# A second edge pass with two sum tables, the last matrix product moved behind the sums, and half of the one-hots on GpSimd

## The chip, the cores and the metric

One core of one Trainium2 chip runs the whole program. The metric is the device time of one execution in microseconds (us). The kernel before has a median of 10212.68 us over 3 runs (10212.11 to 10216.0).

## What is computed

Four graph layers follow one another on 6250 nodes and 106250 edges (100000 drawn ones and a loop per node), each followed by a layer norm of `x + layer(x)`. Only the third layer is touched here:

```python
ef = jnp.concatenate([x[row], x[col], edge_attr], axis=-1)
h = ef @ W1 + b1                              # one row of 128 per edge
mu = jnp.mean(h, axis=0)
var = jnp.mean((h - mu) ** 2, axis=0)
h = (h - mu) * jax.lax.rsqrt(var + BN_EPS) * gamma + beta
h = jax.nn.relu(h)
msgs = h @ W2 + b2
sums = jax.ops.segment_sum(msgs, row, num_segments=n_nodes)
counts = jax.ops.segment_sum(jnp.ones((msgs.shape[0],), dtype=msgs.dtype), row, num_segments=n_nodes)
out = sums / (counts + 1.0)[:, None]
return out + x
```

## The kernel before

The third layer works on edges sorted by source node. Every tile of 128 edges lies inside one block of 128 source nodes; there are 880 tiles, 16 in an iteration (55 iterations, `ITERS2`), and four tiles make a quad. A first pass, `edge_hidden`, computes `h` for every edge, stores it channel by edge in the DRAM table `t_hidden`, and collects the moments. `batch_norm_rows` turns the moments into one scale and one shift per channel. The second pass, `scatter_by_source`, is the one that is changed; then `after_block2` finishes the layer and prepares the fourth one.

In the second pass every quad `q` goes through five steps, each on its own engine, tied by semaphores:

- SP loads 8 tiles (two quads) of `t_hidden` into `rows`, one buffer for each half of the iteration (L2004).
- ACT applies scale, shift and ReLU to the four tiles of a quad (`activate`, L2011), and later copies the quad's messages from PSUM to SBUF (`keep`, L2017).
- PE multiplies each tile by W2, which turns it to edge by channel (`layer`, L2077), and then multiplies it by the tile's one-hot, edge by node of the block, which sums the messages of each node (`add_up`, L2086).
- DVE makes the four one-hots of a quad in one comparison of 128x512 (`match`, L2040), and adds the four 128x128 results to the table `summed` at the column where the tile's node block begins (`add`, L2052). Neighbouring tiles often belong to the same block, so every add waits for the one before it.
- The columns come from `bases`, which loads eight of them at once into DVE's registers (L484), twice in an iteration, ahead of the comparison of that quad.

The order on each engine is written out by hand. DVE: [bases], match(q+1), add(q). ACT: activate(q+1), keep(q). PE: layer(q+1), add_up(q). PSUM holds two quads of each kind, so add_up(q) waits for the adds of quad q-2. GpSimd is idle in this pass.

`after_block2` goes over 7 groups of 7 blocks. DVE joins the sums, the bias times the count, the division and `x` (L2136 to L2143) and runs the layer norm (L820 to L834, its square root on ACT, L841); PE turns the rows (L2195), makes the root product (L2201) and 14 banks of messages (L2208); ACT copies the rows (L2165, L2168), the root product (L2170) and the banks (L2157) and issues the store of the group to DRAM (L2174), for whose end the next group's bank copies wait.

Of the kernel before, what the change touches and what calls it, by code (L numbers as in the profile page):

```python
# [1978 lines left out]
def scatter_by_source(nc, m, a):  # L1979

    with ExitStack() as ctx:
        sb, pb, sem = place(nc, ctx, "sc")
        w2 = sb("w2", [P, C])
# [7 lines left out]
        relued, made, kept, hot_ready, added, window_used = (  # L1991
            [sem(f"{n}{q}") for q in range(QUADS)] for n in ("relued", "made", "kept", "hot_ready", "added", "window_used"))
        w_in, cleared = sem("w_in", "cleared")
        block = ctx.enter_context(nc.Block())
        places = m.iota[:].rearrange("p (a n) -> p a n", a=1).to_broadcast([P, QU, P])

        @block.sync
        def _(sp):
            sp.dma_start(w2[:], a["L2_gnn_W2"]).then_inc(w_in, 16)
# [7 lines left out]
        def _(act):  # L2007
# [10 lines left out]

            activate(0, 0)
# [11 lines left out]

        @block.vector
        def _(dve):
            nc.vector.memset(m.summed[:], 0.0).then_inc(cleared, 1)
            dve.wait_ge(cleared, 1)

            def match(it, q):
                dve.wait_ge(added[q], it)
                low = m.low[:, bass.ds(it * U + q * QU, QU)].rearrange("p (t a) -> p t a", a=1).to_broadcast([P, QU, P])
                nc.vector.tensor_tensor(hot[:, q], places, low, ALU.is_equal).then_inc(hot_ready[q], 1)  # L2040

            def add(it, q, base):
# [21 lines left out]
            for q in range(QUADS):  # L2064
                if q % 2 == 0:
                    base = bases(nc, m.block_base, (ITERS2 - 1) * U + q * QU, DVE, (NT - 1) * P)
                if q < QUADS - 1:
                    match(ITERS2 - 1, q + 1)
# [341 lines left out]
```

## Time and profile before

| | us |
|---|---|
| median of 3 runs | 10212.68 |
| the profiled execution, its own time | 10201.99 |
| its span | 10199.8 |
| second edge pass, loop and ends (8373.0 to 8924.3 of the span) | 551 |
| `after_block2` (8924.3 to about 9095) | 171 |

Engine shares over the whole span: PE 66%, DVE 50%, ACT 13%, GpSimd 66%. They are averages over stages with different limits, so the stage of the change is read by itself. Times in rows are from the span's start; a row's mean duration covers an instruction from start to end, while the next one on the same engine may start before that end, so a pace is read from the distance of starts.

### The profile page before, as it was taken

Reading aid. Unit: us, or ns where it says so; the run is one execution under the profiler, and the core shown is the slowest. Engines: PE = TensorE matmul, PEld = TensorE weight load, DVE = VectorE, ACT = ScalarE, POOL = GpSimd, SP = SyncE. Lnnn points to the kernel's source line nnn. Section 1 sums busy time; section 2 is a strip of 40 time slices with the busy share of each in tenths; the row PEclk is TensorE's granted clock in tenths of the full one; section 3 lists DMA queues with packets and bytes.
Section 4 is the critical chain, followed back from the end, with each engine's and each line's share of the span. In section 5 each row is a group of like instructions: output and inputs, shape, how many; then the busy total and the mean of one; then the engine's idle time right before and its main releaser. Section 6 shows DMA issues by size and latency. Waiting matters only on the chain. (4 is left out here: it accounts for less than half of the span.)

```text
span 10199.8 us, 143982 instructions
## 1 busy us (share of the span) xinstructions
PE 6706.4 (66%) x31287; PEld 5127.7 (50%) x31287; DVE 5144.5 (50%) x16272; ACT 1308.2 (13%) x3084; POOL 6692.3 (66%) x7546
## 2 busy tenths in 40 slices
PE   2787755556677896705888746665566668866665
PEld 1666533334566654404777524444455557733343
DVE  6555655554455534665777434444222226644445
ACT  0000000000000015700000100001122225530000
POOL 1777647777777777767777777773577750027775
PEclk8666655556666685557999955556677779975555
DMA  1222112222333330004777512222566663332222
GB/s 53 52 52 52 45 49 50 51 51 62 98 104 104 104 106 17 2 10 138 220 219 220 169 35 52 52 52 55 146 187 184 185 148 106 100 121 52 52 52 53
DMA packets 556744, 932.76 MB, mean 91 GB/s; under 512 B 161514, under 2 KB 336326, under 8 KB 556302
## 3 DMA queue, kind: packets, MB, share of 16 engines
q0 software_dynamic: 271264, 606.93, 22.5%
q1 hardware_dynamic: 279038, 299.48, 9.4%
q10 hardware_dynamic: 6384, 25.69, 0.6%
q8 instruction: 22, 0.36, 0.0%
q14 instruction: 36, 0.29, 0.0%
HBM read 788.54 MB, written 143.03 MB: 91 GB/s over the span
## 5 line engine op out<-in xcount | busy, mean ns | idle before, releaser
L728 PE MATMUL sage_window<-sage_hot,sage_message 128*128 128x128 f32 x4992 | 1450.2, 433 | 751.7 <-DMA sage_message<-t_x,sage_index_stage 307.2
L728 PEld LDWEIGHTS sage_window<-sage_hot,sage_message 128*128 128x128 f32 x4992 | 1087.5, 297 | 1114.5 <-issue 615.6
L728 PE MATMUL block_window<-block_hot,block_message 128*128 128x128 f32 x3328 | 1186.8, 457 | 672.6 <-DMA block_message<-t_rel,block_index_stage 345.3
L728 PEld LDWEIGHTS block_window<-block_hot,block_message 128*128 128x128 f32 x3328 | 787.3, 294 | 1047.3 <-issue 657.5
L668 DVE TENSOR_TENSOR first_acc<-first_acc,sage_window 128x128 f32 (+1 forms) x1664 | 590.9, 355 | 874.2 <-PE sage_window L728 867.7
L1871 POOL DMA_INDIRECT eh_message<-t_q,eh_stage x880 | 832.2, 946 | 251.9 <-issue 233.9
L578 POOL DMA_INDIRECT sage_message<-t_x,sage_index_stage x832 | 817.4, 982 | 237.6 <-issue 222.1
L728 PE MATMUL gat_window<-gat_hot,gat_message 128*128 128x128 f32 x6656 | 848.0, 281 | 187.7 <-DVE gat_hot L586 96.8
L578 POOL DMA_INDIRECT gat_message<-t_h,gat_index_stage x832 | 793.6, 954 | 237.5 <-issue 222.1
L578 POOL DMA_INDIRECT sage_message<-t_s,sage_index_stage x832 | 788.9, 948 | 237.5 <-issue 222.1
L578 POOL DMA_INDIRECT rgcn_message<-t_rel,rgcn_index_stage x832 | 788.8, 948 | 237.5 <-issue 222.1
L578 POOL DMA_INDIRECT block_message<-in_x,block_index_stage x832 | 787.3, 946 | 237.5 <-issue 222.0
L578 POOL DMA_INDIRECT block_message<-t_rel,block_index_stage x832 | 786.9, 946 | 237.6 <-issue 222.1
L728 PE MATMUL rgcn_window<-rgcn_hot,rgcn_message 128*128 128x128 f32 x1664 | 614.3, 480 | 463.3 <-DMA rgcn_message<-t_rel,rgcn_index_stage 295.3
L728 PEld LDWEIGHTS gat_window<-gat_hot,gat_message 128*128 128x128 f32 x6656 | 782.5, 192 | 249.3 <-issue 106.2
L577 POOL TENSOR_TENSOR all_carrier<-all_ones_i 1x1 int32<-1x1 int32 x624 | 124.4, 199 | 1138.2 <-ACT block_index_stage L565 947.2
L728 PEld LDWEIGHTS rgcn_window<-rgcn_hot,rgcn_message 128*128 128x128 f32 x1664 | 415.1, 313 | 657.9 <-issue 492.2
L1924 PE MATMUL eh_ps<-eh_hot,eh_window 128*128 128x128 f32 x1760 | 481.2, 367 | 389.5 <-DMA eh_message<-t_q,eh_stage 377.7
L1908 DVE TENSOR_SCALAR_CACHE_REDUCE eh_hot<-eh_low_rows,all_column 128x128 f32<-128x128 bf16 x880 | 243.4, 342 | 883.2 <-DMA eh_low_rows<-t_low 883.2
L1924 PEld LDWEIGHTS eh_ps<-eh_hot,eh_window 128*128 128x128 f32 x1760 | 377.3, 265 | 463.8 <-issue 457.5
L784 POOL DMA_INDIRECT t_rec<-attention_records,all_position x420 | 455.0, 1083 | 192.4 <-issue 128.9
L586 DVE TENSOR_SCALAR gat_hot<-all_iota,all_rel,all_alpha 128x128 f32<-128x128 f32 x1680 | 518.5, 362 | 69.6 <-issue 69.5
(474 smaller groups left out, 11121.3 us busy)
## 6 DMA issues: line engine op xcount, KB each, us to landing
eh_window<-t_p SPq DMA_DIRECT2D x880, 64.0 KB
t_hidden<-eh_hidden SPq DMA_DIRECT2D x110, 512.0 KB
sc_rows<-t_hidden SPq DMA_DIRECT2D x110, 512.0 KB, 3.6
eh_low_rows<-t_low SPq DMA_DIRECT2D x110, 256.0 KB, 3.5
t_rel<-n_h ACTq DMA_DIRECT2D x7, 3584.0 KB
eh_message<-t_q,eh_stage POOLq DMA_INDIRECT x880
block_message<-in_x,block_index_stage POOLq DMA_INDIRECT x832, 2.5
sage_message<-t_x,sage_index_stage POOLq DMA_INDIRECT x832, 2.5
```

Source lines behind the costliest of these rows:

```text
L577: nc.gpsimd.tensor_tensor(m.carrier[:], m.ones_i[:], m.ones_i[:], ALU.add).then_inc(e.carried, 1)
L578: pool.indirect_dma_start(message[u][:], None, table, bass.IndirectOffsetOnAxis(ap=stage[h][:, k:k + 1], axis=0)).then_inc(e.gathered[u], 16)
L586: ins = nc.vector.tensor_scalar(hot[:, u, k * P:(k + 1) * P], m.iota[:], m.rel[:, t], weights[k][:, t], ALU.is_equal, ALU.mult)
L668: nc.vector.tensor_tensor(window, window, ps[k][:], ALU.add).then_inc(e.window_used, 1)
L728: last = nc.tensor.matmul(ps[k][:, b, :], message[u][:, f:f + P], hot[:, u, j * P:(j + 1) * P], start=(j == 0), stop=(j == heads - 1))
L784: pool.indirect_dma_start(m.t_rec, bass.IndirectOffsetOnAxis(ap=m.position[:, t0 + n:t0 + n + 1], axis=0), records[:, n, :], None).then_in ...
L1871: pool.indirect_dma_start(message[:, u, :], None, m.t_q, bass.IndirectOffsetOnAxis(ap=stage[h][:, k:k + 1], axis=0)).then_inc(gathered[u / ...
L1908: nc.vector.tensor_scalar(hot[:, q, e], rows, m.column[:], 0.0, ALU.is_equal, ALU.add, accum_out=m.of_source[:, bass.ds(it * U + q * QU + ...
L1924: nc.tensor.matmul(ps[q][:, e], window[:, u, :], hot[:, q, e], start=False, stop=False, skip_group_check=True)
```

## The change

Four edits to the second pass, and what they need in `after_block2`:

- Tiles 0 and 2 of a quad add to `summed`, tiles 1 and 3 to a second table `of_odd`; an add waits for the one two places before it. A second memset clears `of_odd`, and one addition over 128x6272 joins the tables at the end.
- W2 is applied to the summed rows: in the pass PE only turns each tile (`turn`), and `add_up` has its operands exchanged, so that the tables hold channel by node. In `after_block2` ACT copies a group of sums (`first`), PE multiplies its seven blocks by W2 (`project`), and DVE reads the products from PSUM. W2 is loaded there.
- `bases` is issued behind `match` of the same quad instead of ahead of it.
- DVE compares two tiles of a quad (128x256); GpSimd makes the other two, one instruction of 128x128 each, from a copy of eight keys that ACT makes for each half (`stage`), behind a 1x1 addition on `m.carrier`.

```diff
+            def stage(it, h):
+                for q in (2 * h, 2 * h + 1):
+                    act.wait_ge(hot_pool[q], 2 * it)
+                nc.scalar.copy(low[:, h], m.low[:, bass.ds(it * U + h * HU, HU)]).then_inc(staged[h], 1)
...
                     keep(it, q)
+                    if q % 2 == 1:
+                        stage(it + 1, q // 2)
...
+        @block.gpsimd
+        def _(pool):
+            with pool.Fori(0, ITERS2, 1) as it:
+                for q in range(QUADS):
+                    pool.wait_ge(carried, it * QUADS + q)
+                    pool.wait_ge(staged[q // 2], it + 1)
+                    pool.wait_ge(added[q], it)
+                    nc.gpsimd.tensor_tensor(m.carrier[:], m.ones_i[:], m.ones_i[:], ALU.add).then_inc(carried, 1)
+                    for k in range(2, QU):
+                        u = q % 2 * QU + k
+                        nc.gpsimd.tensor_scalar(hot[:, q, k], m.iota[:], low[:, q // 2, u:u + 1], None, ALU.is_equal).then_inc(hot_pool[q], 1)
+
         @block.vector
         def _(dve):
             nc.vector.memset(m.summed[:], 0.0).then_inc(cleared, 1)
-            dve.wait_ge(cleared, 1)
+            nc.vector.memset(of_odd[:], 0.0).then_inc(cleared, 1)
+            dve.wait_ge(cleared, 2)
 
             def match(it, q):
                 dve.wait_ge(added[q], it)
-                low = m.low[:, bass.ds(it * U + q * QU, QU)].rearrange("p (t a) -> p t a", a=1).to_broadcast([P, QU, P])
-                nc.vector.tensor_tensor(hot[:, q], places, low, ALU.is_equal).then_inc(hot_ready[q], 1)
+                key = m.low[:, bass.ds(it * U + q * QU, 2)].rearrange("p (t a) -> p t a", a=1).to_broadcast([P, 2, P])
+                nc.vector.tensor_tensor(hot[:, q, 0:2], places, key, ALU.is_equal).then_inc(hot_dve[q], 1)
 
             def add(it, q, base):
                 dve.wait_ge(added[q], it + 1)
                 for k in range(QU):
-                    if k == 0 and q == 0:
+                    if k < 2 and q == 0:
                         dve.wait_ge(window_used[QUADS - 1], QU * it)
-                    elif k == 0:
-                        dve.wait_ge(window_used[q - 1], QU * (it + 1))
+                    elif k < 2:
+                        dve.wait_ge(window_used[q - 1], QU * it + 3 + k)
                     else:
-                        dve.wait_ge(window_used[q], QU * it + k)
-                    window = m.summed[:, bass.ds(base[(q % 2) * QU + k], C)]
-                    nc.vector.tensor_tensor(window, window, ps_a[q % 2][:, k, :], ALU.add).then_inc(window_used[q], 1)
+                        dve.wait_ge(window_used[q], QU * it + k - 1)
+                    table = (m.summed, of_odd)[k % 2]
+                    nodes = table[:, bass.ds(base[(q % 2) * QU + k], C)]
+                    nc.vector.tensor_tensor(nodes, nodes, ps_a[q % 2][:, k, :], ALU.add).then_inc(window_used[q], 1)
...
                 for q in range(QUADS):
-                    if q % 2 == 0:
-                        base = bases(nc, m.block_base, it * U + q * QU, DVE, (NT - 1) * P)
                     if q < QUADS - 1:
                         match(it, q + 1)
                     else:
                         match(it + 1, 0)
+                    if q % 2 == 0:
+                        base = bases(nc, m.block_base, it * U + q * QU, DVE, (NT - 1) * P)
                     add(it, q, base)
...
+            dve.wait_ge(window_used[QUADS - 1], QU * ITERS2)
+            chain(dve, m)(nc.vector.tensor_tensor(m.summed[:], m.summed[:], of_odd[:], ALU.add))
 
         @block.tensor
         def _(pe):
-            def layer(it, q):
+            def turn(it, q):
                 pe.wait_ge(relued[q], it + 1)
                 pe.wait_ge(*bank_before(kept, it, q))
                 for k in range(QU):
-                    last = nc.tensor.matmul(ps_m[q % 2][:, k, :], relu[:, q, k * P:(k + 1) * P], w2[:], start=True, stop=True)
+                    last = nc.tensor.transpose(ps_m[q % 2][:, k, :], relu[:, q, k * P:(k + 1) * P], m.ident[:])
                 last.then_inc(made[q], 1)
...
-                    last = nc.tensor.matmul(ps_a[q % 2][:, k, :], hot[:, q, k, :], message[:, q, k, :], start=True, stop=True)
+                    last = nc.tensor.matmul(ps_a[q % 2][:, k, :], message[:, q, k, :], hot[:, q, k, :], start=True, stop=True)
                 last.then_inc(added[q], 1)
...
-                    nc.vector.scalar_tensor_tensor(y[:, j, :], b2[:], m.out_degree[:, 0, node], m.summed[:, bass.ds((g * GN + j) * C, C)],
+                    nc.vector.scalar_tensor_tensor(y[:, j, :], b2[:], m.out_degree[:, 0, node], ps[:, j, :],
                                                    ALU.mult, ALU.add).then_inc(joined, 1)
...
+            def first(g):
+                act.wait_ge(made, g)
+                nc.scalar.copy(sums[:].rearrange("p j n -> p (j n)"), m.summed[:, group_cols(g)]).then_inc(staged, 1)
...
             with act.Fori(0, NG - 1, 1) as g:
+                first(g + 1)
                 take(g, range(EARLY))
...
+            def project(g):
+                pe.wait_ge(staged, g + 1)
+                pe.wait_ge(root_taken, g)
+                for j in range(GN):
+                    last = nc.tensor.matmul(ps[:, j, :], sums[:, j, :], w2[:], start=True, stop=True)
+                last.then_inc(made, 1)
...
+            project(0)
             root_term(0)
             with pe.Fori(0, NG - 1, 1) as g:
+                project(g + 1)
                 messages(g)
                 root_term(g + 1)
```

## Rows read from the trace of the kernel before

**Rows 1.** Stretches, loop of the pass and `after_block2`: PE, PEld, DVE, ACT, POOL busy; clock

```profile
8383.50:8921.40 537.90, 444.24 (x3496) 406.35 (x3494) 373.66 (x1095) 281.46 (x435) 0.00 (x0) 1.00 0.36 104
8929.30:9095.00 165.70, 116.26 (x273) 52.88 (x273) 64.51 (x271) 75.59 (x128) 0.18 (x2) 0.86 0.38 155
```

**Rows 2.** Groups by line, 8377 to 8925: count, busy us, mean ns, idle before

```profile
L2052 DVE TENSOR_TENSOR by_source_summed<-by_source_summed,sc_ps_a 128x128 f32 x880 | 251.8, 286 | 89.0 <-PE sc_ps_a L2086 2.2 <-DVE by_source_summed L2052 0.2
L2086 PE MATMUL sc_ps_a<-sc_message,sc_hot 128*128 128x128 f32 x1760 | 251.2, 286 | 93.2 <-issue 74.2 <-DVE sc_hot L2040 18.9
L2077 PE MATMUL sc_ps_m<-sc_w,sc_relu 128*128 128x128 f32 x1760 | 234.1, 276 | 6.9 <-ACT sc_relu L2011 6.9
...
L2011 ACT ACTIVATE sc_relu<-sc_rows,all_norm 128x512 f32<-128x512 f32 x220 | 179.4, 816 | 11.0 <-DMA sc_rows<-t_hidden 11.0
L2040 DVE TENSOR_TENSOR sc_hot<-all_iota,edges_low 128x512 f32<-128x512 f32 x220 | 151.4, 688 | 78.0 <-issue 78.0
L2017 ACT COPY sc_message<-sc_ps_m 128x512 f32<-128x512 f32 x220 | 128.7, 585 | 254.8 <-PE sc_ps_m L2077 254.8
```

**Rows 3.** Instructions in order of time, DVE, one iteration: start, duration

```profile
8601.75 0.69 DVE L2040 TENSOR_TENSOR sc_hot<-all_iota,edges_low 128x512 f32<-128x512 f32 x1
8602.35 1.54 DVE L2052 TENSOR_TENSOR by_source_summed<-by_source_summed,sc_ps_a 128x128 f32 x4
8604.46 0.69 DVE L2040 TENSOR_TENSOR sc_hot<-all_iota,edges_low 128x512 f32<-128x512 f32 x1 [0.57 <-issue]
...
8609.53 0.69 DVE L2040 TENSOR_TENSOR sc_hot<-all_iota,edges_low 128x512 f32<-128x512 f32 x1 [0.86 <-issue]
```

**Rows 4.** One line's instructions (L484) in that iteration, min/median/max ns

```profile
L484 DVEq TENSOR_LOAD <-edges_block_base x2: 595/596/596, 8603.7 to 8608.8; - x2
```

**Rows 5.** In order of time, PE, the loop's first quads

```profile
8384.13 1.06 PE L2086 MATMUL sc_ps_a<-sc_message,sc_hot 128*128 128x128 f32 x8
8385.02 1.06 PE L2077 MATMUL sc_ps_m<-sc_w,sc_relu 128*128 128x128 f32 x8
```

**Rows 6.** In order of time, PE: seven transposes at granted clock 1.00, seven at about 0.5

```profile
8957.72 0.93 PE L2195 MATMUL n_ps_t<-all_ident,n_x 128*128 128x128 f32 x7
...
8364.94 1.73 PE L1972 MATMUL bn_ps_t<-all_ident,edges_of_source 128*128 128x128 f32 x7 [6.80 <-PEq L799]
```

**Rows 7.** In order of time, DVE: an unchained addition from PSUM and its follower

```profile
3706.45 0.28 DVE L1232 TENSOR_TENSOR n_f_out<-n_ps_fa,first_sage_bias_f 128x128 f32<-128x128 f32 x1
3706.64 0.15 DVE L1233 COPY all_al<-n_ps_fa 128x4 f32<-128x4 f32 x1
```

**Rows 8.** One line's instructions: DVE comparison of two SBUF inputs, min/median/max ns

```profile
L1376 DVE TENSOR_TENSOR al_high_hot<-all_iota,all_src_high x208: 350/352/415, 3900.9 to 4314.8; 128x196 f32<-128x196 f32 x104
```

**Rows 9.** One line's instructions, GpSimd: the 1x1 addition and an indirect DMA

```profile
L1870 POOL TENSOR_TENSOR all_carrier<-all_ones_i x110: 181/181/183, 7225.2 to 8326.8; 1x1 int32<-1x1 int32 x110
L1871 POOL DMA_INDIRECT eh_message<-t_q,eh_stage x880: 940/944/967, 7225.8 to 8336.2; - x176
```

**Rows 10.** One line's instructions: landing of the row loads (L2004); ACT copy 128x8

```profile
DMA to landing us min/median/max: 3.4/3.6/4.4
L1877 ACT COPY eh_stage<-edges_dst x110: 192/195/197, 7224.9 to 8326.5; 128x8 int32 x108, 128x8 int32<-128x8 int32 x2
```

**Rows 11.** One line's instructions: whole-table operations on DVE

```profile
L2034 DVE MEMSET by_source_summed<- x1: 5285/5285/5285, 8374.5 to 8374.5; 128x6272 f32 x1
L882 DVE TENSOR_TENSOR degrees_ends<-degrees_ends,all_ident x1: 6692/6692/6692, 1279.3 to 1279.3; 128x6272 f32<-128x6272 f32 x1
```

**Rows 12.** In order of time, ACT and PE in `after_block2`, one group

```profile
8986.69 0.91 ACT L2170 COPY third_acc<-n_ps 128x896 f32 x1 [3.43 <-PE n_ps L2201]
8991.25 3.24 ACT L2157 COPY n_h<-n_ps_h 128x512 f32<-128x512 f32 x6 [3.66 <-DMA t_rel<-n_h]
8991.89 8.85 PE L2208 MATMUL n_ps_h<-n_w,n_x_t 128*128 128x512 f32 x20 [1.68 <-ACT n_h L2157]
```

**Rows 13.** Stretch of the first edge pass, columns as in rows 1

```profile
7400.00:7500.00 100.00, 64.94 (x344) 55.48 (x343) 22.20 (x160) 26.16 (x90) 76.99 (x91) 0.78 0.63 188
```

More of the change, by code:

```diff
@@ L1982, in scatter_by_source @@
         sb, pb, sem = place(nc, ctx, "sc")
-        w2 = sb("w2", [P, C])
         rows = sb("rows", [P, 2, HU * P])
@@ L1990, in scatter_by_source @@
         rows_in = [sem(f"rows_in{h}") for h in range(2)]
-        relued, made, kept, hot_ready, added, window_used = (
-            [sem(f"{n}{q}") for q in range(QUADS)] for n in ("relued", "made", "kept", "hot_ready", "added", "window_used"))
-        w_in, cleared = sem("w_in", "cleared")
+        low, of_odd = sb("low", [P, 2, HU]), sb("of_odd", [P, ROWS])
+        relued, made, kept, hot_dve, hot_pool, added, window_used = (
+            [sem(f"{n}{q}") for q in range(QUADS)] for n in ("relued", "made", "kept", "hot_dve", "hot_pool", "added", "window_used"))
+        staged = [sem(f"staged{h}") for h in range(2)]
+        cleared, carried = sem("cleared", "carried")
         block = ctx.enter_context(nc.Block())
-        places = m.iota[:].rearrange("p (a n) -> p a n", a=1).to_broadcast([P, QU, P])
+        places = m.iota[:].rearrange("p (a n) -> p a n", a=1).to_broadcast([P, 2, P])
         @block.sync
         def _(sp):
-            sp.dma_start(w2[:], a["L2_gnn_W2"]).then_inc(w_in, 16)
             with sp.Fori(0, ITERS2, 1) as it:
@@ L2017, in keep @@
                 nc.scalar.copy(message[:, q], ps_m[q % 2][:]).then_inc(kept[q], 1)
+            def stage(it, h):
+                for q in (2 * h, 2 * h + 1):
+                    act.wait_ge(hot_pool[q], 2 * it)
+                nc.scalar.copy(low[:, h], m.low[:, bass.ds(it * U + h * HU, HU)]).then_inc(staged[h], 1)
+            for h in range(2):
+                stage(0, h)
             activate(0, 0)
@@ L2062, in _ @@
                         match(it + 1, 0)
+                    if q % 2 == 0:
+                        base = bases(nc, m.block_base, it * U + q * QU, DVE, (NT - 1) * P)
                     add(it, q, base)
             for q in range(QUADS):
+                if q < QUADS - 1:
+                    match(ITERS2 - 1, q + 1)
                 if q % 2 == 0:
                     base = bases(nc, m.block_base, (ITERS2 - 1) * U + q * QU, DVE, (NT - 1) * P)
-                if q < QUADS - 1:
-                    match(ITERS2 - 1, q + 1)
                 add(ITERS2 - 1, q, base)
+            dve.wait_ge(window_used[QUADS - 1], QU * ITERS2)
+            chain(dve, m)(nc.vector.tensor_tensor(m.summed[:], m.summed[:], of_odd[:], ALU.add))
         @block.tensor
         def _(pe):
-            def layer(it, q):
+            def turn(it, q):
                 pe.wait_ge(relued[q], it + 1)
@@ L2081, in add_up @@
                 pe.wait_ge(kept[q], it + 1)
-                pe.wait_ge(hot_ready[q], it + 1)
+                pe.wait_ge(hot_dve[q], it + 1)
+                pe.wait_ge(hot_pool[q], 2 * (it + 1))
                 used, times = bank_before(window_used, it, q)
@@ L2085, in add_up @@
                 for k in range(QU):
-                    last = nc.tensor.matmul(ps_a[q % 2][:, k, :], hot[:, q, k, :], message[:, q, k, :], start=True, stop=True)
+                    last = nc.tensor.matmul(ps_a[q % 2][:, k, :], message[:, q, k, :], hot[:, q, k, :], start=True, stop=True)
                 last.then_inc(added[q], 1)
-            pe.wait_ge(w_in, 16)
-            layer(0, 0)
+            turn(0, 0)
             with pe.Fori(0, ITERS2 - 1, 1) as it:
@@ L2093, in _ @@
                     if q < QUADS - 1:
-                        layer(it, q + 1)
+                        turn(it, q + 1)
                     else:
-                        layer(it + 1, 0)
+                        turn(it + 1, 0)
                     add_up(it, q)
@@ L2099, in _ @@
                 if q < QUADS - 1:
-                    layer(ITERS2 - 1, q + 1)
+                    turn(ITERS2 - 1, q + 1)
                 add_up(ITERS2 - 1, q)
@@ L2174, in store @@
                 act.dma_start(node_rows(m.t_rel8, g, R8 * C), h[:].rearrange("p j r n -> p j (r n)")).then_inc(stored, 16)
+            first(0)
             second(0)
```

8 lines of the change are left out of this document (5 added, 3 removed).

## The prediction

> **What bounds the kernel now.** The page's shares (PE 66%, DVE 50%) say nothing about this stage, so I read the stretches first. In the loop of the second edge pass PE is busy 444 of 538 us at a granted clock of 1.00, DVE 374, ACT 281, GpSimd none [rows 1]. PE looks like the bound. The groups by line correct that: the adds on DVE waited for PE 2.2 us in all, and the 78 us before comparisons and most of the 89 us between adds have no other engine behind them, while PE idled 93 us before `add_up` [rows 2]. DVE in order of time settles it [rows 3]: a comparison starts at 8601.75, its quad of adds at 8602.35, and the next comparison at 8604.46, where it sat idle 0.57 us; at the loop's end it is 0.86. From 8601.75 to the same place an iteration later are 9.84 us. So DVE is the bound, through latency as much as work: four adds take 1.54 us, 4 x 0.286 of work and three gaps of 0.13 [rows 2, 3] where an add waits for the one before. The two longer idles hold a register load of 0.596 us [rows 4] that starts at 8603.7, with the last add, and at 8608.8.
>
> The profiled execution took 10201.99 us, the median is 10212.68: I make the sum against the first and add the 10.7 at the end.
>
> **The change part by part.** I work out an iteration of 16 tiles for every engine; the longest counts, and all else is paid once or in `after_block2`.
>
> *DVE, adds.* An add that waits for the one two places back may start when that has ended, 0.286 + 0.13 = 0.42 us after its start, so two adds share 0.42. Unchained, such an addition from PSUM is followed after 0.19 us [rows 7]. Both give 0.21 an add, 0.84 a quad against a start-to-start 1.45 now (8602.35 plus 1.54, less the overlap of 0.09 with the next comparison). Bounds: 0.19, and 0.42 if they still ran one by one.
>
> *DVE, comparisons.* 128x512 takes 0.69, the next instruction follows after 0.60 [rows 3]; 128x196 takes 0.35 [rows 8], so an element costs 0.00107 us, and 128x256 takes 0.42, followed after 0.34. A quad is 0.34 + 0.84 = 1.18 us, four are 4.7.
>
> *DVE, bases behind the comparison.* The load needs 0.6 us of the sequencer and started about 0.1 after the last add. Behind `match` it starts a little later but runs while that add and the comparison (0.21 + 0.34) execute; the adds need it. What stays uncovered is about 0.4 us in mid-iteration and 0.65 at the loop's branch, where the load starts 0.3 later. The two now cost 0.65 and 0.95 (9.84 less four times 2.06 of a plain quad). DVE: 4.7 + 1.05 = 5.8 us an iteration.
>
> *PE.* Unhindered, four matmuls (eight records) start 0.89 us after the previous four [rows 5]. Seven transposes take 0.93 us at full clock, one record each, so 0.11 us a transpose [rows 6]: `turn` is 0.45. A quad is 1.34, an iteration 5.4 (now 7.1). The exchange of operands in `add_up` changes no size; I cost it at nothing.
>
> *ACT.* ReLU 0.816 and copy 0.585 [rows 2] overlap their followers by 0.1 each, 1.2 us a quad; two stagings of 0.195 [rows 10] come on top: 5.2 us. `stage` waits for GpSimd's previous use of the keys; queued behind that wait are the next ReLU, the copy PE waits for, and so all of it, if GpSimd lags. An iteration's distance should cover it.
>
> *GpSimd.* No compute instruction of size runs on it in this trace. Below lies the 1x1 addition of 0.181, above the indirect DMA of 0.944 [rows 9]. DVE does a 128x128 addition in 0.286. I take 0.5, between the small one and twice DVE's: a quad is 0.181 + 2 x 0.5 + 0.15 for waits, about 1.3, an iteration 5.3. By the ends it is 2.8 or 8.9. The Trainium skill (GPSIMD Engine Reference, side-by-side cycle accounting) has about 2.6 cycles an element at 1.2 GHz, by which the work of 128 columns would be an estimated 0.28 us and the instruction near 0.46; no run here shows it.
>
> *DVE against GpSimd.* Comparisons on DVE while GpSimd is busy with DMA issues ran 350/352/415 ns [rows 8], so hardly a delay, but GpSimd read nothing from SBUF there. I leave 0 to 0.3 us a comparison and take 0.1. The Trainium skill (SBUF: two separate sides) says that a DVE instruction with two SBUF inputs and a GpSimd instruction that reads SBUF exclude one another for their whole length. The comparison has two such inputs; by that rule an average wait could be 0.12 us and the worst 0.5; the row cannot decide it.
>
> *The row loads.* A half's buffer is reloaded when ReLU has consumed it, and a load lands 3.6 us after issue (3.4 to 4.4) [rows 10]. Now three quads (7.4 us) hide that. After the change a cycle of the buffer is 0.2 + 3.6 + 0.1 for load and hand-over, then 0.7 + 0.5 + 0.2 + 0.8 of ReLU, copy, staging, ReLU: 6.1 us. This is late next together with DVE.
>
> So DVE has 5.8 + 0.4 = 6.2, the loads 6.1, PE 5.4, GpSimd 5.3, ACT 5.2. With that many near one another I add 0.3 for them missing each other: 6.5 us, in a plausible band of 5.8 to 7.2. Saved: 55 x (9.84 - 6.5) = 184 us (145 to 222).
>
> *Paid once.* The second memset stands before the first comparison: 5.3; the joining addition has the size of L882: 6.7, and 0.2 for its wait [rows 11]. Together 12.2.
>
> *after_block2.* Group 0 now begins with an ACT copy of 128x896 (0.91 [rows 12]), 7 matmuls at half clock (7 x 0.44) and hand-overs: 4.3. In the first loop pass PE can start its messages only behind copy and product (0.9 + 7 x 0.22 + hand-overs, perhaps part at half clock): 3.5. In the other five ACT waits 3.66 us for the store anyway, which hides copy and product; what goes is PE's head start, so that the first six bank copies, 0.53 us apart now, run at PE's pace, 20 records in 8.85 us or 0.86 a bank [rows 12]: 6 x 0.33 = 2 each, 10. One more weight load: 0.4. Sum 18 (8 if the wait hides all, 26 if nothing).
>
> Total: -184 + 12 + 18 = -154, so 10048 for the profiled execution and 10059 us for the median.
>
> **The rivals.**
>
> GpSimd sets the pace. Its instruction would have to take over 0.65 us; against it speaks that its 1x1 instruction shows a fixed part of only 0.18, for it that no large one is seen and that it may be kept out of SBUF by DVE. At 0.8 the quad is 2.0 and the iteration 8.0: -101 + 30, 10142 us.
>
> The adds stay one by one in effect, because the registers and waits ahead of each fill the gap: 4 x (0.34 + 1.45) + 1.05 = 8.2 us: 10153. Against it: register work ahead of an add is a small part of its 0.13 gap, and the follower in rows 7 came after 0.19.
>
> PE's clock falls, and the kernel is slower. In the first edge pass, PE busy 65% of the time between waits for gathers, the granted clock is 0.78, a mix of 2.4 and 1.2 GHz [rows 13]. If the loop ran at 1.2 throughout, transposes would be 0.22 us apart [rows 6] and matmuls 0.44: 16 x 0.66 = 10.6 us an iteration, 0.7 more than now. 55 x 0.7 + 30 = +69: 10281 us. It decides from 9.3 us an iteration on, a mean clock near 0.58. Against it: PE stays busy 80% and its idles stay under about 1 us; in the loop before, with 83% busy, it is 1.00 [rows 1], and the transposes of [rows 6] ran at full clock behind matmuls. The Trainium skill (TensorE: Matmul & The Clock Gate, Part 4: PE-mode transpose) says that transposes do not engage the full clock; by that only `add_up` would speak for it here.
>
> The transposes save nothing (0.89 a quad as before): PE 7.1, with hand-overs 7.3: 10103, inside the range. All overlaps work and the stores hide `after_block2`: 5.6 us, 10001.
>
> **How the numbers follow.** Forecast with its band 0.62, GpSimd 0.14, chained adds 0.07, transposes no cheaper 0.05, better than the band 0.06, clock 0.06. The range of 8 in 10 goes from 10005, the band's lower end with the cheaper `after_block2`, to 10155, which takes in the rivals on GpSimd and the adds; it leaves out a fully lowered clock and part of both tails. About 0.2% is what a measurement of this kernel can tell from no change. Only the clock, and GpSimd near its upper bound (8.9 us plus exclusion), reach that side: faster 0.92, same 0.02, slower 0.06.
>
> **What would show it.** Starts of same-place comparisons 6.5 us apart; adds 0.21 apart; `turn` 0.45 with one record a tile; ACT's ReLU waiting now and then for the row loads; GpSimd instructions under 0.6 us; granted clock 1.00; DVE idle 5 us longer at the start, a 6.7 us addition at the end; the group pace in `after_block2` 2 us longer. Wrong: a DVE comparison stretched well over 0.42 us, ACT waiting for GpSimd in `stage`, a clock under 0.9, or `after_block2` over 26 us longer.

## The result and the profile after

| | before | after |
|---|---|---|
| median | 10213.83 us (4 runs, 10212.11 to 10216.0) | 10043.4 us (4 runs, 10038.81 to 10044.24) |
| ratio | | 0.9832, 95% interval 0.9815 to 0.9849 |
| iteration of 16 tiles | 9.84 us | 6.19 us |
| second pass, first clearing to the end of the last add or join | 548.4 us | 361.2 us |
| from there to the first instruction of the next stage on DVE | 171.2 us | 189.1 us |

The change took 170.4 us, 16 more than the forecast's 154; the forecast was 10059 with 10005 to 10155 as its range. The pass gave 187.2 us and the stage behind it took back 17.9. The two profiled executions differ by 158 us only, because the gathers ahead of the pass, which nothing changed, ran slower in the one of after (a median of 947 ns for an indirect DMA instead of the 944 of [rows 9], with nearly 6000 of them ahead of the pass; the first clearing starts at 8384.6 instead of the 8374.5 of [rows 11]). That fits the 10.7 us by which the profiled execution of before lay under its median, while the one of after (10043.6) lies on its own.

The two stretches as in [rows 1], loop of the pass and `after_block2`: PE, PEld, DVE, ACT, POOL busy, granted clock, DMA share, GB/s.

```profile
8393.50:8740.00 346.50, 321.91 (x2632) 296.54 (x2632) 281.83 (x1102) 292.24 (x541) 294.32 (x648) 0.99 0.55 162
8757.50:8934.80 177.30, 127.42 (x357) 63.46 (x357) 63.22 (x266) 81.62 (x132) 0.00 (x0) 0.86 0.35 145
```

All five are now busy 81 to 93% of the pass, and the granted clock stays at its upper level, 2.4 GHz.

The groups by line of the pass, 8387 to 8750 (count, busy us, mean ns, idle before them and what ended it), against [rows 2]:

```profile
L2052 POOL TENSOR_SCALAR sc_hot<-all_iota,sc_low 128x128 f32<-128x128 f32 x436 | 255.6, 594 | 3.2
L2113 PE MATMUL sc_ps_a<-sc_hot,sc_message 128*128 128x128 f32 x1760 | 244.5, 282 | 25.8 <-issue 12.1 <-DVE sc_hot L2063 7.2
...
L2012 ACT ACTIVATE sc_relu<-sc_rows,all_norm 128x512 f32<-128x512 f32 x220 | 179.3, 815 | 3.6 <-DMA sc_rows<-t_hidden 3.6
L2103 PE MATMUL sc_ps_m<-all_ident,sc_relu 128*128 128x128 f32 x880 | 133.2, 275 | 6.4 <-ACT sc_relu L2012 6.4
L2018 ACT COPY sc_message<-sc_ps_m 128x512 f32<-128x512 f32 x220 | 128.9, 586 | 52.6 <-PE sc_ps_m L2103 49.5
L2076 DVE TENSOR_TENSOR by_source_summed<-by_source_summed,sc_ps_a 128x128 f32 x440 | 125.6, 285 | 53.0 <-PE sc_ps_a L2113 52.4 <-issue 0.6
L2076 DVE TENSOR_TENSOR sc_of_odd<-sc_of_odd,sc_ps_a 128x128 f32 x440 | 123.5, 281 | 0.2 <-DVE by_source_summed L2076 0.2
...
L2063 DVE TENSOR_TENSOR sc_hot<-all_iota,edges_low 128x256 f32<-128x256 f32 x220 | 102.0, 464 | 11.4 <-issue 11.4
```

PE's idle ahead of `add_up` fell from 93 us to 26, the transposes are 880 records in place of 1760, and ACT waited for a row load once, 3.6 us. DVE has 53 us of idle ahead of its adds, which the row puts down to PE. DVE in order of time (start, duration), one iteration, against [rows 3], shows that it was something else:

```profile
8560.32 0.42 DVE L2063 TENSOR_TENSOR sc_hot<-all_iota,edges_low 128x256 f32<-128x256 f32 x1 [0.21 <-issue]
8561.33 0.29 DVE L2076 TENSOR_TENSOR by_source_summed<-by_source_summed,sc_ps_a 128x128 f32 x1 [0.59 <-PE sc_ps_a L2113]
8561.54 0.28 DVE L2076 TENSOR_TENSOR sc_of_odd<-sc_of_odd,sc_ps_a 128x128 f32 x1
8561.75 0.29 DVE L2076 TENSOR_TENSOR by_source_summed<-by_source_summed,sc_ps_a 128x128 f32 x1
8561.96 0.29 DVE L2076 TENSOR_TENSOR sc_of_odd<-sc_of_odd,sc_ps_a 128x128 f32 x1
8562.16 0.42 DVE L2063 TENSOR_TENSOR sc_hot<-all_iota,edges_low 128x256 f32<-128x256 f32 x1
8562.50 0.28 DVE L2076 TENSOR_TENSOR by_source_summed<-by_source_summed,sc_ps_a 128x128 f32 x1
...
8563.31 0.51 DVE L2063 TENSOR_TENSOR sc_hot<-all_iota,edges_low 128x256 f32<-128x256 f32 x1
8564.16 0.29 DVE L2076 TENSOR_TENSOR by_source_summed<-by_source_summed,sc_ps_a 128x128 f32 x1 [0.34 <-PE sc_ps_a L2113]
...
8564.99 0.50 DVE L2063 TENSOR_TENSOR sc_hot<-all_iota,edges_low 128x256 f32<-128x256 f32 x1
...
8566.51 0.42 DVE L2063 TENSOR_TENSOR sc_hot<-all_iota,edges_low 128x256 f32<-128x256 f32 x1 [0.21 <-issue]
```

The adds start 0.21 us apart. Where no register load stands between comparison and adds (8562.16), the first add follows after 0.34. Where one does, it follows after 1.01 (quad 0) and 0.85 (quad 2). The load was under way then:

```profile
L484 DVEq TENSOR_LOAD <-edges_block_base x2: 594/596/599, 8563.4 to 8566.6; - x2
```

It starts 0.1 us after the comparison (0.04 in quad 2) and runs 0.6. So the iteration is 1.84 + 1.15 + 1.68 + 1.52 us on DVE. In quad 0 nothing but the load is late: PE's matmuls for the adds at 8567.51 had ended by 8566.97 (start 8565.82, 1.15 long). In quad 2 the load ends at 8563.95 and PE's matmuls at 8563.92 (8562.77 and 1.15), so this one iteration does not tell them apart. The loop does: in every iteration of this trace the first add of quad 2 starts 0.21 us behind the end of the load, to within 2 ns, and it is the same 0.21 in s1, u3 and l4 (below), where PE's matmuls had ended 0.19 or 0.28 us before the add instead of 0.24. In quad 0 it is 0.31 us in all of them, and in l16. So the load held the adds in both quads, and most of the 53 us is its doing, although the profile puts them down to PE. All iterations but the first and the last take 6.18 to 6.20 us.

PE in order of time, where `turn` (one record a tile) and `add_up` (two) alternate:

```profile
8563.76 0.60 PE L2103 MATMUL sc_ps_m<-all_ident,sc_relu 128*128 128x128 f32 x4
8564.20 1.06 PE L2113 MATMUL sc_ps_a<-sc_hot,sc_message 128*128 128x128 f32 x8
8565.09 0.60 PE L2103 MATMUL sc_ps_m<-all_ident,sc_relu 128*128 128x128 f32 x4
```

A turn is 0.44 us from start to start, an `add_up` 0.89, and so 5.3 us an iteration.

What is paid once (min/median/max ns and starts, as in [rows 11]):

```profile
L2057 DVE MEMSET sc_of_odd<- x1: 5285/5285/5285, 8391.1 to 8391.1; 128x6272 f32 x1
L2095 DVE TENSOR_TENSOR by_source_summed<-by_source_summed,sc_of_odd x1: 6691/6691/6691, 8739.1 to 8739.1; 128x6272 f32<-128x6272 f32 x1
```

The second clearing starts 6.5 us after the first, not 5.3: 1.26 us of idle stand between them.

In `after_block2`, ACT's groups by line (8750 to 8935):

```profile
L2185 ACT COPY n_h<-n_ps_h 128x512 f32<-128x512 f32 x98 | 56.4, 588 | 50.5 <-PE n_ps_h L2249 33.8 <-DMA t_rel<-n_h 16.3
L2189 ACT COPY n_sums<-by_source_summed 128x896 f32 (+1 forms) x7 | 6.6, 940 | 16.9 <-PEq L799 16.9
```

The bank copies waited 16.3 us for the stores and 33.8 for PE. The new copy has no wait in the loop, and the seven take 6.6 us.

### The profile page after: what moved, and what is told of

Same layout as the page of the kernel before. It is cut to its first block and busy times, and to the rows that moved or that the text cites. A ratio compares the mean times of both kernels' runs of the same rounds, so it can differ in the third digit from the quotient of the medians.

```text
span 10041.8 us, 144438 instructions
## 1 busy us (share of the span) xinstructions
PE 6609.5 (66%) x30505; PEld 5035.7 (50%) x30505; DVE 5067.5 (50%) x16274; ACT 1327.1 (13%) x3201; POOL 7003.6 (70%) x8206
## 5 line engine op out<-in xcount | busy, mean ns | idle before, releaser
L589 DVE TENSOR_SCALAR sage_hot<-all_iota,all_rel 128x128 f32<-128x128 f32 x1680 | 490.8, 293 | 122.5 <-issue 122.4
```

Source lines behind the costliest of these rows:

```text
L589: ins = nc.vector.tensor_scalar(hot[:, u, :], m.iota[:], m.rel[:, t], None, ALU.is_equal)
```

## The experiments

u1 to u4 undo one part each, v1 puts one part alone into the kernel before, s1, s2, l4 and l16 take a suspected cost or wait away or change its size, and a1, b1 and b2 repeat the change and go beyond it. The runs were on different chips. On two of them the stages with gathers are slower, so that the kernel before takes 12713 to 12734 us instead of 10214. The pass itself runs alike everywhere (6.19 us an iteration in the first run of the change, 6.18 in a1), so an iteration (same-place comparison to comparison, the median of the loop) is compared by itself, and totals only on one chip. All but a1, b1 and b2 are single runs. For u1 to u4 the whole kernel took 12701.21, 12614.31, 12579.21 and 12619.10 us, beside 12732.79 for the kernel before; for s1, s2, l4 and l16 it took 10038.65, 10012.44, 10024.84 and 10060.81, beside 10202.04.

**u1: one table again.** Every add waits for the one before. The second table is still cleared and joined, so that the loop alone differs. The two waits of a quad's first adds go back to one as well:

```diff
...
-                    elif k < 2:
-                        dve.wait_ge(window_used[q - 1], QU * it + 3 + k)
+                    elif k == 0:
+                        dve.wait_ge(window_used[q - 1], QU * (it + 1))
                     else:
-                        dve.wait_ge(window_used[q], QU * it + k - 1)
-                    table = (m.summed, of_odd)[k % 2]
+                        dve.wait_ge(window_used[q], QU * it + k)
+                    table = m.summed
```

> The changed kernel with one edit undone: all adds go to one table and each waits for the one before (the second table is still cleared and joined). If overlapping adds are worth what the prediction said, four adds go from 0.84 back to 1.45 us start to start and the iteration from 6.18 to about 4 x (0.34 + 1.45) + 1.2 = 8.4 us: the pass 120 us longer, the kernel near 10165 us. Rival: the loop is held by something else at 6.18 (row loads, ACT, GpSimd), and most of the 2.4 us an iteration is absorbed: an iteration under 7.2 us, under 10100 us.

Measured: 8.67 us an iteration (8.66 between the comparisons at 10902.25 and 10910.91), a little over the 8.4, and the rival's 7.2 fell. The second table is worth 2.48 us of it, 136 us in 55 iterations. It is the largest part.

**u2: the load ahead of the comparison again.**

```diff
+                    if q % 2 == 0:
+                        base = bases(nc, m.block_base, it * U + q * QU, DVE, (NT - 1) * P)
                     if q < QUADS - 1:
                         match(it, q + 1)
                     else:
                         match(it + 1, 0)
-                    if q % 2 == 0:
-                        base = bases(nc, m.block_base, it * U + q * QU, DVE, (NT - 1) * P)
...
```

> The changed kernel with the register load ahead of the comparison again. Now 0.67 + 0.51 + 0.21 us an iteration stay uncovered beside the load; ahead of the comparison it should be 0.65 + 0.95, so 0.2 to 0.3 us an iteration more (6.4 to 6.5 us), 10 to 16 us in all, about 10056 us. Rival: PE or ACT sets the pace and the place of the load is worth nothing: 6.2 us, 10043.

Measured: 7.21 us, 1.0 more than the change, where 0.2 to 0.3 had been expected. DVE in order of time, two quads:

```profile
10902.53 0.28 DVE L2076 TENSOR_TENSOR sc_of_odd<-sc_of_odd,sc_ps_a 128x128 f32 x1
10903.68 0.53 DVE L2063 TENSOR_TENSOR sc_hot<-all_iota,edges_low 128x256 f32<-128x256 f32 x1 [0.86 <-issue]
...
10904.95 0.42 DVE L2063 TENSOR_TENSOR sc_hot<-all_iota,edges_low 128x256 f32<-128x256 f32 x1
10905.66 0.29 DVE L2076 TENSOR_TENSOR by_source_summed<-by_source_summed,sc_ps_a 128x128 f32 x1 [0.29 <-PE sc_ps_a L2113]
```

The comparison comes 0.86 us late, then the adds of the following quad wait 0.21 to 0.29 for PE. PE stands idle 0.64 and 0.70 us ahead of the two `add_up`s that need the late comparisons. So a load ahead of a comparison delays PE too, and a load behind it delays only adds whose input is ready. The expectation had counted DVE's time alone.

**u3: all one-hots on DVE.** GpSimd and the staging copies are idle; the comparison is 128x512 again.

> The changed kernel with all four one-hots of a quad on DVE in one comparison of 128x512, GpSimd and the staging copies gone. DVE is the bound: 0.26 us more a quad, of which the longer comparison hides some of the register load in two of four: +0.5 to +1.0 us an iteration, less 0.17 of exclusion that goes: 6.6 to 7.0 us, 25 to 45 us longer, about 10078. Rival: GpSimd and its exclusion with DVE hold the loop now, and without it an iteration is no longer than 6.2.

Measured: 6.64 us (10901.49 to 10908.13), as expected: GpSimd's half is worth 0.45 us, 25 us in all. The longer comparison (0.69 instead of 0.42) costs nothing in the two quads with a load, which are as long as in the change (1.84 and 1.67 us), because the load starts and ends where it did; the other two are 0.27 and 0.18 longer. That is why it is not 4 x 0.26.

**u4: W2 in the pass again.** The four transposes become matmuls with W2, `add_up` stays as it is, and `project` multiplies the sums by the identity.

> The changed kernel with W2 multiplied inside the pass again instead of the transposes; after it the sums are multiplied by the identity, so that all else stays as it is. PE needs 8 x 0.89 = 7.1 us an iteration and becomes the bound: 7.1 to 7.4 us, 50 to 67 us longer, about 10100. Rival: matmuls and transposes cost PE the same or PE has slack: 6.2 us, 10043.

Measured: 7.15 us, PE without a gap, 0.89 for each step:

```profile
10902.25 1.06 PE L2116 MATMUL sc_ps_a<-sc_hot,sc_message 128*128 128x128 f32 x8
10903.14 1.06 PE L2106 MATMUL sc_ps_m<-sc_w,sc_relu 128*128 128x128 f32 x8
```

The transposes are worth 0.96 us an iteration, 53 us. They only pay because the other parts have brought DVE under PE's 7.15.

**v1: the two tables alone in the kernel before.** With the waits, the second clearing and the joining addition of the change:

```diff
...
-                    window = m.summed[:, bass.ds(base[(q % 2) * QU + k], C)]
+                    window = (m.summed, of_odd)[k % 2][:, bass.ds(base[(q % 2) * QU + k], C)]
...
```

> The kernel before with one part of the change alone: even and odd tiles add to two tables, which are joined at the end. If the second table takes 0.13 us from each of the sixteen adds whatever else is in the pass, its iteration goes from 9.84 to 9.84 - 2.1 = 7.7 us (7.6 to 8.0), still over TensorE's 7.15: with 55 iterations 117 us less, and 13 us more once for the second clearing and the join. Rival (the parts only pay together, because in the kernel before VectorE's other work and TensorE's matmuls with W2 take up what the adds leave): 8.5 to 9.2.

Measured: 7.45 us (10899.80, 10907.25, 10914.70), 2.39 less than before, 131 us. This is below the expected 7.6 to 8.0: the expectation took 0.13 us from each add, but four adds went from 1.45 to 0.84 us, 0.15 each. One part of four brings two thirds of the loop's gain. Removing the parts one by one costs 136 + 56 + 25 + 53 = 270 us, more than the 201 that the loop gained: they share limits, so the prices do not add up. The whole kernel took 12609.17 us in its one run, against 12722.06 for the kernel before.

**s1: GpSimd idle.** 

> This kernel leaves out one-hots 2 and 3 of every quad (their tiles are set to zero once, before the loop), with the staging copies and the carrier tile of GpSimd: GpSimd has nothing to do in the pass, and ScalarE two copies less per iteration. Theory (VectorE sets the iteration, GpSimd only stretches it): the comparison goes from 0.50 back to 0.42 when nothing runs beside it, and at most 2 x 0.08 of stretched comparisons go: 6.0 to 6.1 us per iteration instead of 6.185. Rival (GpSimd's chain sets it in effect, through the one-hots that TensorE waits for, as in the forecast's rival of GpSimd's pace): 5.4 to 5.7.

Measured: 6.23 us (8562.24 to 8568.47), not less than 6.19: both the theory's 6.0 to 6.1 and the rival's 5.4 to 5.7 fell. The comparison did go back to its own length:

```profile
L2048 DVE TENSOR_TENSOR sc_hot<-all_iota,edges_low x206: 416/418/427, 8400.2 to 8719.8; 128x256 f32<-128x256 f32 x103
```

In the changed kernel the same line has a mean of 464 ns and at most 597, and the four comparisons of an iteration differ: 0.42 and 0.43 in two, 0.50 and 0.51 in the others. In the iteration shown above GpSimd's comparisons ran beside the short ones for 0.19 and 0.25 us and beside the long ones for 0.44 and 0.47; the row of POOL beside the comparison at 8564.99 is

```profile
8564.26 1.17 POOL L2052 TENSOR_SCALAR sc_hot<-all_iota,sc_low 128x128 f32<-128x128 f32 x2
```

So DVE is held up a little beside GpSimd's comparisons, by 0.04 us in the mean and 0.18 at most. Of the four quads the first three are as long in s1 as in the change (1.84, 1.15 and 1.67 us), as the load or the comparison's 0.42 sets them. Only the last differs: in the change its first add follows the stretched comparison after 0.41 us (8564.99), and in s1 it follows the short one after 0.45 (8566.90), because there it starts 0.13 us behind the end of PE's matmuls. GpSimd's delay is there, but without it a wait as long stands in its place.

**s2: the columns loaded once, before the loop.**

```diff
+            base = bases(nc, m.block_base, 0, DVE, (NT - 1) * P)
             with dve.Fori(0, ITERS2 - 1, 1) as it:
...
-                    if q % 2 == 0:
-                        base = bases(nc, m.block_base, it * U + q * QU, DVE, (NT - 1) * P)
...
```

> The registers with the column numbers are loaded once, ahead of the loop, so every iteration adds to the columns of the first half iteration: the output is that of other places, the amount of adding is the same. Theory (each exposed load costs VectorE about 0.6 us twice per iteration, and VectorE sets the pace): 6.185 minus 2 x (1.01 - 0.2) leaves 4.7 to 5.0 of VectorE, under ScalarE's 5.45 and TensorE's 5.4: the iteration comes to 5.4 to 5.6. Rival (the cycle of the row loads, 3.9 of landing and the wait for the relus, holds the iteration, as the forecast had it at 6.1): it stays at 6.0 to 6.2, and ScalarE is seen to wait for the DMA. Second rival (the load's place does not matter, the comparison and the adds wait for TensorE anyway): 6.1 to 6.2, with ScalarE and TensorE back to back.

Measured: 5.90 us (5.81 in the iteration from 8561.72 to 8567.53, 5.5 to 6.1 over the loop behind its first iteration), below both rivals and above the theory's 5.4 to 5.6. The loads do hold the iteration in the change, but the next limit lies only 0.3 below. ACT in order of time:

```profile
8563.17 0.57 ACT L2018 COPY sc_message<-sc_ps_m 128x512 f32<-128x512 f32 x1
8563.99 0.81 ACT L2012 ACTIVATE sc_relu<-sc_rows,all_norm 128x512 f32<-128x512 f32 x1 [0.26 <-DMA sc_rows<-t_hidden]
...
8566.97 0.81 ACT L2012 ACTIVATE sc_relu<-sc_rows,all_norm 128x512 f32<-128x512 f32 x1 [0.42 <-DMA sc_rows<-t_hidden]
```

Now the first ReLU of a half waits for its row load, 0.75 us an iteration in all. The row loads (L2005) over the whole loop, who waited for them (us, times) and their time to landing:

```profile
ACT sc_relu L2012: 44.5, 77
DMA to landing us min/median/max: 3.4/3.5/4.5
```

This limit is the cycle of the buffer that the forecast had at 6.1 us. Measured from one load of a half to the next, in medians over the loop: 3.55 us to landing, 0.02 until ReLU starts, 2.10 to the end of the half's second ReLU, 0.22 until the next load is issued. The sum of 5.89 is the iteration, with no other wait in it, and its spread is that of the landings.

**l4 and l16: four columns a load, or sixteen.** 

> Four columns are loaded in every quad instead of eight in every second one. If a load's time is per register (0.596 for 8, so 0.3 for 4), it fits under the 0.42 comparison and no quad has its stretch of 1.01 from comparison to add: 5.5 to 5.8 us per iteration. If a load has one fixed time of about 0.6, four quads have that stretch: 6.185 + 2 x 0.16, and with what TensorE waits in turn 6.5 to 7.1.

> Sixteen columns are loaded once per iteration. If a load has one fixed time of about 0.6, one exposed stretch of two goes: 5.9 to 6.1 us per iteration. If its time is per register (1.2 for 16), quad 0 has 0.6 more, more than the other quad gives back: 6.3 to 6.7.

Measured: l4 6.17 us (6.19 from 8561.94 to 8568.13), l16 6.73 (6.72 from 8563.24 to 8569.96). The load of each, first l4, then l16:

```profile
L484 DVEq TENSOR_LOAD <-edges_block_base x4: 341/345/365, 8562.0 to 8566.5; - x4
```

```profile
L484 DVEq TENSOR_LOAD <-edges_block_base x1: 1101/1101/1101, 8563.3 to 8563.3; - x1
```

With 596 for eight that is 0.063 us a register and 0.095 fixed, so the first alternative of each expectation was right about the load. For l16 the time came out too, at the upper end (6.3 to 6.7); for l4 it didn't (5.5 to 5.8). The reason is in DVE's order of time in l4:

```profile
8561.94 0.42 DVE L2063 TENSOR_TENSOR sc_hot<-all_iota,edges_low 128x256 f32<-128x256 f32 x1 [0.21 <-issue]
8562.69 0.29 DVE L2076 TENSOR_TENSOR by_source_summed<-by_source_summed,sc_ps_a 128x128 f32 x1 [0.33 <-issue]
...
8563.53 0.42 DVE L2063 TENSOR_TENSOR sc_hot<-all_iota,edges_low 128x256 f32<-128x256 f32 x1
8564.16 0.29 DVE L2076 TENSOR_TENSOR by_source_summed<-by_source_summed,sc_ps_a 128x128 f32 x1 [0.22 <-issue]
```

A load of 0.345 sits under the comparison's 0.42, but the first add starts 0.75 and 0.63 us after the comparison and not 0.34. Over the three sizes the distance at the loop's branch is 0.75, 1.01 and 1.51: the load's own time plus 0.41 each time, 0.1 before the load and 0.31 behind it. Beyond the 0.34 the quads of an iteration lose 0.41 + 0.29 + 0.26 + 0.26 = 1.2 us in l4, 0.67 + 0.51 = 1.2 in the change, 1.17 in l16. Sixteen registers cost about 1.2 us however they are cut, nearly the loads' own length: what the comparison hides, the hand-over around the load (0.25 to 0.28 in all, at the branch 0.41) takes back. In l16 the columns are at hand in the other quads, and it still loses 0.5 more: after the long gap another quad's adds wait 0.33 us for PE, and the comparison behind them is stretched to 0.60.

**a1, b1, b2: the change again, and two versions beyond it.** b1 takes away what is paid once: the odd tiles' table is the accumulator of the next stage, DVE clears both tables behind the last comparison of the first edge pass, and makes the sums of a group in `after_block2`.

```diff
+            nc.vector.memset(m.summed[:], 0.0).then_inc(cleared, 1)
+            nc.vector.memset(m.acc[:, 0, 0:ROWS], 0.0).then_inc(cleared, 1)
...
-            chain(dve, m)(nc.vector.tensor_tensor(m.summed[:], m.summed[:], of_odd[:], ALU.add))
...
-                nc.scalar.copy(sums[:].rearrange("p j n -> p (j n)"), m.summed[:, group_cols(g)]).then_inc(staged, 1)
...
+                nc.vector.tensor_tensor(sums[:].rearrange("p j n -> p (j n)"), m.summed[:, group_cols(g)], m.acc[:, 0, group_cols(g)], ALU.add).then_inc(staged, 1)
```

b2 adds another order in `after_block2`:

```diff
-                project(g + 1)
-                messages(g)
+                messages(g, range(4))
+                project(g + 1)
+                messages(g, range(4, BANKS))
                 root_term(g + 1)
```

> The changed kernel once more, as it is, to stand beside the next two in the same rounds: 0.982 to 0.985 of the kernel before.

> The changed kernel without its costs paid once: both tables are cleared by VectorE behind its last comparison of the pass before (where the trace has it idle for 12.5 us until the batch norm), the sum of the two tables is made group by group by VectorE in the next stage (about 1.1 us each, in place of ScalarE's copy of 0.94), and the odd tiles' table is the later stage's accumulator. Expected: 8.5 us earlier first add, less at most 1.2 us by which the clearing outlasts the last store of the pass before, 6.7 us of the join, and 0 to 3 us from ScalarE's copies: 14 to 17 us less than the changed kernel, the iteration of the pass unchanged at 6.19. Rival (the stage waits for its first row load and the weight load of the next stage anyway, so that clearing and join were partly covered): 5 to 9 us less.

> b1 and, in the stage behind the pass, another order: ScalarE copies the turned rows ahead of the kept ones, TensorE makes the first four banks of messages of a group before it projects the next group with W2, and the rows are stored in two halves, so that the first half's buffer is free when the next group's first banks come. The group of 20.8 us has TensorE busy for 16.6; expected is a group of 17.9 to 18.5, six times 2.3 to 2.9: 14 to 17 us less than b1. Rival (the store's landing, about 10 us for a group, sets when ScalarE may copy, whatever TensorE's order): less than 4 us in all.

| | median | range (4 runs) | last comparison of the first pass to the last bank copy, start to start |
|---|---|---|---|
| a1 | 12555.13 us | 12525.24 to 12557.59 | 560.6 us |
| b1 | 12535.9 us | 12532.3 to 12550.1 | 544.2 us |
| b2 | 12520.6 us | 12509.02 to 12524.75 | 531.1 us |

Against the 12722.06 of the kernel before these are ratios of 0.9859 (0.9843 to 0.9876), 0.9851 (0.9835 to 0.9868) and 0.9837 (0.9821 to 0.9854). a1's 167 us are the 170 of the first chip on a longer kernel, so that its ratio lies just outside the expected 0.982 to 0.985. The intervals overlap; the stretch in the last column separates the three: b1 gives 16.4 us and b2 13.2 more.

b1 is as expected in the sum (14 to 17), but by luck, as two of its parts are off and cancel. The first add comes 2.8 us earlier than in a1, counted from the last comparison of the first pass, where 7.3 were expected: 1.26 us of idle stand ahead of each clearing, and the batch norm starts 4.4 us later than in a1. In `after_block2` the first to the last bank copy take 136.1 us, as before the change, and 143.4 in the change: ACT's copy of the sums cost 7.4 us, where 0 to 3 were expected. The rest is mostly the join (6.7), less 0.8 us by which the loop is longer.

b2's 13.2 misses its 14 to 17 by a little, up to the last bank copy. To the first DVE instruction of the next stage it is 18.1, because only half a group's rows are left to store: 6.3 us lie between the last bank copy and that instruction, and 11.2 in b1. PE's time for a group fell from 20.5 to 18.9 us in most groups, not to 18.5, as PE now waits for the layer norm:

```profile
11136.16 0.98 PE L2237 MATMUL n_ps_t<-all_ident,n_x 128*128 128x128 f32 x7 [1.46 <-DVE n_x L834]
11138.27 1.77 PE L2243 MATMUL n_ps<-n_x_t,n_w 128*128 128x448 f32 x4 [1.13 <-ACT n_x_t L2196]
11139.88 3.60 PE L2250 MATMUL n_ps_h<-n_w,n_x_t 128*128 128x512 f32 x8
```

The store's rival fell: with two halves ACT does not wait for it. b2 is the fastest kernel of this study, some 30 us under the change in that stretch and 34.5 in the median.

## Why the prediction was right

**The bound.** DVE stayed the bound, as forecast: the load, the comparison or the adds set every quad of its iteration. The step "6.2 for DVE, and 0.3 for them missing each other" gave 6.5; it was 6.19. The loop gained 55 x 3.65 = 201 us where 184 were forecast, and this is nearly all of the difference to the result.

**Adds.** 0.21 us apart, as worked out from 0.286 + 0.13 over two. u1 and v1 put 2.4 to 2.5 us an iteration on it.

**Comparisons.** 0.42 long and followed after 0.34, as from [rows 3] and [rows 8], where GpSimd does not stretch them.

**The bases.** Here a term was too small. The forecast left 1.05 us uncovered, 0.4 and 0.65; the trace has 0.51 and 0.67 between comparison and add, and 0.21 more of idle at the branch: 1.4 us. The step "runs while that add and the comparison (0.21 + 0.34) execute" failed in part: the load starts 0.1 behind the comparison and not with the last add, and l4 and l16 show that it delays the adds by nearly its whole length. Moving it was still worth 1.0 us (u2), by way of PE.

**DVE against GpSimd.** The 0.4 us of the sum (0.1 a comparison) were too much. The comparison is stretched by 0.04 in the mean, and s1 shows no gain when GpSimd is idle. The rule of the Trainium skill (SBUF — State Buffer, section SBUF: two separate sides) that such a pair of instructions exclude one another for their whole length would have allowed waits up to GpSimd's 0.59. The longest comparison is 0.18 over its own length, and the one at 8564.99 ran beside a GpSimd comparison for 0.44 of its 0.50 us, so the trace shows less than that.

**The missing each other.** The 0.3 us were not needed: the too-small bases (1.05 for 1.4) and the too-large 0.4 and 0.3 partly cancel, 5.8 + 0.35 = 6.15 against 6.19. The sum came out better than its terms, and that is luck.

**PE.** 5.3 us an iteration for the forecast's 5.4, and the exchange of operands cost nothing (0.89 a quad in both, [rows 5]). u4 has the rival "the transposes save nothing" at 7.15 an iteration, near its 7.3; it did not happen, the transposes took half of a matmul with W2.

**ACT.** 5.45 us an iteration (6.19 less idles of 0.32 and 0.42) for the forecast's 5.2; it never waited for GpSimd's use of the keys.

**The row loads**, forecast at 6.1, did not hold 6.19. With the register loads away they are the limit (s2), at 5.9: the mechanism was right and the 6.1 some 0.2 too much.

**GpSimd.** Its comparison takes 0.594 us, not 0.5. A quad of 0.2 + 1.17 is under 1.55, so the rival of GpSimd's pace, which needed 0.65, stayed away by little; s1, with GpSimd idle and the iteration no shorter, shows that it did. The estimate of 0.46 from the Trainium skill (GPSIMD Engine Reference, section Elementwise — side-by-side cycle accounting) was further off; the page measured its 2.6 cycles an element on an instruction with two inputs.

**The clock.** The rival slower than before asked for a granted clock under 0.58; it was 0.99 to 1.00. The rule of the Trainium skill (TensorE: Matmul & The Clock Gate, Part 4: PE-mode transpose) that transposes do not engage the full clock changed nothing here: they are a third of the records, between matmuls, and the clock stayed at 2.4 GHz.

**Paid once.** 6.5 + 6.7 = 13.2 us for the forecast's 12.2; what was missed is the 1.26 us of idle between two memsets.

**after_block2.** 17.9 us for 18. From the end of the sums to the first joined product it is 4.9 us more (forecast 4.7 with the weight load), from there to the first bank copy 5.6 more (forecast 3.5), and from the first to the last bank copy 7.3 (forecast 10): the copy and the product lie in front of PE's messages in every group, as forecast, and a shorter wait for the store hid 6.7 us (23.0 us before, 16.3 after). Here too the sum is better than its terms. b1, where the product is still in front but ACT's copy is gone, has none of the 7.3: it was the copy.

**The offset.** Adding the 10.7 us between profiled execution and median was right: the gathers of that execution were quicker, and the change itself was forecast at 154 us and measured at 170. Without them the forecast would have been 10048, nearer to the 10043 measured, but by luck only. Two ends were added up a little off: the band's lower end with the cheaper `after_block2` gives 10011 and not 10005, and 5.6 us an iteration gives 10000 and not 10001.

## What to carry to other kernels

Where accumulations into one table wait for one another, two tables and one joining pass give back the gap of each pair; it was two thirds of the loop's gain here, and it can be had alone. Then read the order on the engine that is the bound for small things that delay another engine: a register load cost nearly its own length here even behind a comparison, and ahead of one it made the other engine wait too, so put it behind whatever the other engine waits for. What a restructuring pays once may be free in a neighbouring stage: b1 got back 16.4 of the 13.2 + 17.9 us. And where a wait is put down to an engine that had been done for half a microsecond, look at what the sequencer did in between: the distance from the end of the load, the same in five kernels, showed the cause that the profile had put down to another engine.

## What the runs showed of the hardware

A load into DVE's registers took 0.345, 0.596 and 1.101 us for 4, 8 and 16 registers, and the first add that uses them came 0.41 us plus that length after the start of the comparison ahead (0.25 to 0.28 where no loop branch stands between). Two memsets of 5.285 us with no dependence on one another stood 1.26 us apart on DVE, in two places. Comparisons with two SBUF inputs ran 0.42 us beside an idle GpSimd and 0.42 to 0.60 beside one that compared 128x128 in 0.594, and an iteration with GpSimd idle was no shorter (6.23 us for 6.19). A load of eight tiles landed 3.4 to 4.5 us after its issue, and with 2.1 us of work on its buffer, the ReLUs' part, a buffer came round every 5.9 us (s2).
